# Attention, gate and output in one block, with later row sums for two chunks

## What is computed

```python
xn = _layernorm(x, axis=-1)
s = _L0_attn_ref(xn, wq, wk, wv, wo)     # softmax(q k^T * 32**-0.5, causal) v, then @ wo
g = _silu(_L0_ffn_ref(xn, W_base, b_base, W_router, lora_A, lora_B))
x = x + s * g                            # ffn: xn @ W_base.T + b + 2 * sum over top-2 experts w_e (xn A_e) B_e
```

## Time and profile before

| | us |
|---|---|
| median of 3 runs | 3402.35 (3400.29 to 3406.72) |
| the profiled execution | 3404.86 |
| its span, first to last instruction | 3403.1 |
| PE busy | 3266.6 |
| DVE busy | 1877.9 |
| ACT busy | 1441.0 |
| POOL busy | 1357.8 |

### The profile page before, as it was taken

The page is one execution under the profiler, slowest core; times in us unless marked ns, Lnnn a source line. Parts: engine busy times, 40 slices in busy tenths (PEclk is TensorE's granted clock), DMA queues, the critical chain, the costliest instruction groups (busy, mean ns, idle before and its releaser), DMA issues. The chain is left out here.

```text
span 3403.1 us, 51307 instructions
## 1 busy us (share of the span) xinstructions
PE 3266.6 (96%) x18048; PEld 2193.0 (64%) x18048; DVE 1877.9 (55%) x4622; ACT 1441.0 (42%) x2658; POOL 1357.8 (40%) x549
## 2 busy tenths in 40 slices
PE   6999999799999999999999999999997999989999
PEld 5888888655555555555555555555552788878887
DVE  5333332287777777777777777777771322223333
ACT  3221121046666666666666666666665211100000
POOL 0000000046766766776676677667666000000000
PEclk9999999899999999999999999999998999999999
DMA  6555554345665656566565656656664544435554
GB/s 229 161 161 159 171 175 143 110 97 123 131 143 124 140 128 135 128 136 143 122 139 130 137 131 131 139 128 137 134 150 114 176 147 140 140 130 194 196 188 171
DMA packets 283503, 494.53 MB, mean 145 GB/s; under 512 B 40864, under 2 KB 156576, under 8 KB 263328
## 3 DMA queue, kind: packets, MB, share of 16 engines
q1 hardware_dynamic: 260256, 333.04, 32.9%
q0 software_dynamic: 20736, 151.00, 22.1%
q10 hardware_dynamic: 2304, 7.87, 0.7%
HBM read 205.03 MB, written 134.74 MB: 100 GB/s over the span
## 5 line engine op out<-in xcount | busy, mean ns | idle before, releaser
L882 POOL TENSOR_TENSOR added<-added,probs 128x2048 f32<-128x2048 f32 (+3 forms) x320 | 1177.0, 3678 | 863.5 <-PE o_ps L953 812.4
L1061 DVE TENSOR_REDUCE row_max<-rows_ps 128x1 f32<-128x512 f32 x1536 | 994.1, 682 | 262.4 <-PE rows_ps L915 259.5
L1035 ACT ACTIVATE probs<-cols_ps 128x512 f32<-128x512 f32 x1728 | 922.3, 610 | 329.1 <-PE cols_ps L997 295.8
L1065 DVE CUSTOM_DVE_ANT_0 masked_rows<-rows_ps,tri 128x128 bf16<-128x128 f32 (+3 forms) x1024 | 482.1, 482 | 221.5 <-PE rows_ps L915 219.1
L915 PE MATMUL rows_ps<-k_st,q_st 96*128 96x512 f32 (+3 forms) x1536 | 527.0, 372 | 26.4 <-DMA q_st<-scratch_q_hi 17.0
L997 PE MATMUL cols_ps<-q_st,k_st 97*128 97x512 f32 x1248 | 519.6, 423 | 0.6
L953 PE MATMUL o_ps<-probs,v_st 128*32 128x512 f32 (+3 forms) x4224 | 429.4, 523 | 0.0
L997 PE MATMUL cols_ps<-q_st_last,k_st 97*128 97x512 f32 x928 | 382.5, 426 | 7.0 <-ACT dma_added L1035 3.1
L915 PEld LDWEIGHTS rows_ps<-k_st,q_st 96*128 96x128 f32 x1536 | 295.3, 193 | 117.0 <-DVE row_max L1061 46.3
L915 PE MATMUL rows_ps<-k_st,q_st_last 96*128 96x512 f32 (+3 forms) x1024 | 366.4, 384 | 2.7 <-DVE row_max L1061 0.4
L997 PEld LDWEIGHTS cols_ps<-q_st,k_st 97*128 97x128 f32 x1248 | 236.6, 190 | 171.2 <-issue 107.4
(11 more groups left out here) (113 smaller groups left out, 3799.9 us busy)
## 6 DMA issues: line engine op xcount, KB each, us to landing
dma_added<-probs POOLq DMA_DIRECT2D x144, 1024.0 KB, 7.4
q_st<-scratch_q_hi SPq DMA_DIRECT2D x96, 256.0 KB, 5.5
x_sb<-in_x SPq DMA_DIRECT2D x32, 512.0 KB, 3.9
scratch_xt_hi<-xt_hi SPq DMA_DIRECT2D x32, 512.0 KB, 6.0
scratch_xt_lo<-xt_lo SPq DMA_DIRECT2D x32, 512.0 KB, 6.7
scratch_q_hi<-out_hi SPq DMA_DIRECT2D x64, 256.0 KB, 2.4
scratch_q_lo<-out_lo SPq DMA_DIRECT2D x64, 256.0 KB, 2.9
l_sb<-scratch_l_inv SPq DMA_DIRECT2D x256, 64.0 KB, 4.3
```

The lines of the kernel that those rows point to most:

```text
L882: nc.gpsimd.tensor_tensor(total[:, :, q0:CH], total[:, :, q0:CH], probs_of(c, j)[:, :, q0:CH], ALU.add).then_inc(pool_added, 1)
L1035: nc.scalar.activation(probs_of(c, j)[:, :, i * P:(i + 1) * P], cols_ps[cols_slot(AT_T[t])][:, :].rearrange("p (h q) -> p h q", h=NREP), A ...
L1061: nc.vector.tensor_reduce(into, bank[:, :], AX.X, ALU.max).then_inc(rows_free, 1)
L1065: nc.vector.tensor_tensor_reduce(masked_rows[rows_slot(k)][:, 0:keys], bank[:, 0:keys], tri[:, CH - keys:CH], 1.0, MASKED, ALU.add, ALU.ma ...
```

## The change

1. **Row sums.** Y of chunks 1 and 2 stands at the second visit of the next chunk, eight tiles later; its normalisation keeps its distances. The semaphore of the adding DMAs is split by the chunk's parity.
2. **One block.** `attend`, `gate` and `output` become one block; the gate's and the output's programs are functions called by each engine behind its attention, or in the tail of it.
3. **Buffers.** The gate's and output's buffers are laid by hand over those of the attention. The split gate weights w[k] (high and low together) take the place of probs 0 to 6, added0 and dma_added0. l_inv is gone: the reciprocal is taken in place.
4. **Tail.** ACT rounds the gate weights at the start of the tail, each as soon as its score buffer is read. DVE makes the remainders and finishes tile 0's silu before the last reciprocal. PE makes tile 0's products before the last row sums. SP loads gate tile 0 in the last group, tile 1 when the last exponential is done, and everything else of the gate behind the tail.
5. **Gate to output.** The load and the split of output tile 0 stand before the last gate tile's silu; tile 1's load waits for the last gate product. The output uses two other banks.

```diff
-    _t = weighed_at((_c + 1) % CPB, 0 if _c else 2) + (0 if _c + 1 < CPB else NTG)
+    _t = weighed_at(_c + 1, 2) if _c + 1 < CPB else weighed_at(0, 0) + NTG
...
+        (ow_hi, o_x0, gw, ow_lo, ow_raw, g_g, o_raw0, g_t1, g_z, _, g_th, g_bias, o_g0) = laid_out(
+            ("ow_hi", [P, KT, D], FP32R), ("o_x0", [P, D], FP32),
+            ("gw", [P, NW, 2, D], FP32R),
...
@@ SP
+                if n.lin(1) == NG and c == 0:
+                    wait_apart(sp, probs_ready, n.lin(NUG, 0), passed)
+                    gate.load(sp, 1, 1)
...
+                            gate.load(sp, 0, 0)
...
             over_stages(run)
-            for s in range(CPB):
-                sp.wait_ge(o_stored[s], 16 + 16 * NG)
-            sp.wait_ge(gw_loaded, 16 * NW)
+            gate.stores_before_last(sp)
+            for s in o_stored:
+                wait_apart(sp, s, 16 + 16 * NG, passed)
+            output.load_first(sp)
+            gate.last_stores(sp, output.load_second)
+            output.loads_and_stores(sp)
@@ PE
                     elif kind == "Y":
+                        if n.lin(1) == NG:
+                            pe.wait_ge(rows_free, NSG * NG + 1)
+                            gate.first_products(pe)
                         row_sums(n, *op[1:])
             over_stages(run)
+            gate.products(pe)
+            output.products(pe)
@@ ACT
+            def split_high(n):
+                act.wait_ge(gw_loaded, 16 * NW)
+                for k in range(NW):
+                    if k < EARLY:
+                        j = next(j for c, j in reversed(RING) if probs_slot(RING.index((c, j))) == k)
+                        act.wait_ge(values_done, weighed_count(n, CPB - 1, 1, j))
+                        if j in ADDS[CPB - 1]:
+                            act.wait_ge(pool_added, n.lin(NADD, adds_through(CPB - 1, j) - NADD))
+                        if j in DMA_ADDS[CPB - 1]:
+                            act.wait_ge(dma_done[1], n.lin(16 * NDMA[1], 16 * (dma_adds_through(CPB - 1, j) - NDMA[1])))
+                    gate.high(act, k)
...
+            gate.tanhs(act, output.first_high)
+            output.highs(act)
@@ DVE
                     elif kind == "I":
                         cc, back = op[1:3]
+                        if n.lin(1) == NG:
+                            gate.lows(dve)
+                            gate.first_silu(dve, cols_full, cols_count(n, AT_Y[cc]))
                         dve.wait_ge(l_moved[cc % 2], n.lin(32, 16 * (cc // 2 + 1) - 32 * back))
-                        nc.vector.reciprocal(l_inv[cc % 2][:, :], l_few[cc % 2][:, :]).then_inc(l_inv_ready, 1)
+                        nc.vector.reciprocal(l_few[cc % 2][:, :], l_few[cc % 2][:, :]).then_inc(l_inv_ready, 1)
...
+            gate.silus(dve, output.first_low)
+            output.finishes(dve)
@@ in last_stores of the gate, SP
+        store(sp, Step(NPAIR - 1, 0))
+        wait_apart(sp, acc_full, 2 * NT, passed)
+        load_second(sp)
+        store(sp, Step(NPAIR - 1, 1))
```

More of the change, by code:

```diff
@@ L17 @@
+from collections import namedtuple
 from contextlib import ExitStack
@@ L552 @@
 NRG = len(RING)
+EARLY = 7
 def probs_slot(g):
@@ L645 @@
 NADD = sum(len(a) - 1 for a in ADDS if a)
-NDMA = sum(len(a) - 1 for a in DMA_ADDS if a)
+NDMA = [sum(len(a) - 1 for a in DMA_ADDS[par::2] if a) for par in range(2)]
 def adds_through(c, j):
@@ L676, in attend @@
         sb("gw_raw_end", [P, D])
+        probs = [sb(f"probs{i}", [P, NREP, CH]) for i in range(EARLY)]
+        added = [sb("added0", [P, NREP, CH])]
+        dma_added = [sb("dma_added0", [P, NREP, CH])]
+        probs += [sb(f"probs{i}", [P, NREP, CH]) for i in range(EARLY, NPROBS)]
+        added.append(sb("added1", [P, NREP, CH]))
+        dma_added.append(sb("dma_added1", [P, NREP, CH]))
         q_st.append(sb("q_st_last", [K1 + 1, NREP, CH], FP32R))
@@ L679, in attend @@
         v_st = [sb(f"v_st{i}", [P, S // P, HD]) for i in range(2)]
+        o_sb = [sb(f"o_sb{i}", [P, CH]) for i in range(CPB)]
+        g_t0 = sb("g_t0", [P, 2, NW, P], FP32R)
         ones = sb("ones", [P, HD])
-        probs = [sb(f"probs{i}", [P, NREP, CH]) for i in range(NPROBS)]
-        added = [sb(f"added{i}", [P, NREP, CH]) for i in range(2)]
-        dma_added = [sb(f"dma_added{i}", [P, NREP, CH]) for i in range(2)]
         row_max = [sb(f"row_max{i}", [P, NREP, TPC, CPB]) for i in range(2)]
@@ L710, in attend @@
         pool_added = sem("a_pool_added")
-        dma_done = sem("a_dma_done")
+        dma_done = [sem(f"a_dma_done{i}") for i in range(2)]
         chunk_copied = sem("a_chunk_copied")
@@ L720, in attend @@
         NW = KT + 1
+        gate = gate_programs(nc, ctx, sc, wo, b_base, gw_raw, gw, ow_raw, ow_hi, ow_lo, [g_t0, g_t1], g_bias, g_z, g_th, g_g,
+                             rows_ps[0:2], passed)
+        output = output_programs(nc, ctx, x, sc, out, ow_hi, ow_lo, [o_raw0, o_raw1], [o_t0, o_t1], [o_x0, o_x1], [o_g0, o_g1],
+                                 o_prod, o_y, rows_ps[2:4], gate, passed)
         block = ctx.enter_context(nc.Block())
@@ L809, in move_row @@
                 sp.dma_start(q_st[c][K1:K1 + 1, :, :].bitcast(FP32), row[c % 2][:, :]).then_inc(row_moved[c % 2], 16)
-            for s in o_stored:
+            for s in o_stored + gate.g_stored:
                 sp.sem_inc(s, 16)
@@ L821, in run @@
             def run(n, c, ops):
-                last_group = isinstance(n.pair, int) and n.lin(1) == NG - 1
+                last_group = n.lin(1) == NG - 1
+                if n.lin(1) == NG and c == 0:
+                    wait_apart(sp, probs_ready, n.lin(NUG, 0), passed)
+                    gate.load(sp, 1, 1)
                 for op in ops:
@@ L866, in run @@
                                          o_sb[cc][:, :]).then_inc(o_stored[cc], 16)
+                            if last_group and cc == 2:
+                                for i in range(2):
+                                    wait_apart(sp, o_stored[i], 16 + 16 * NG, passed)
+                                gate.load_bias(sp)
             over_stages(run)
-            for s in range(CPB):
-                sp.wait_ge(o_stored[s], 16 + 16 * NG)
-            sp.wait_ge(gw_loaded, 16 * NW)
+            gate.stores_before_last(sp)
[4 more added lines that the diff above has]
+            output.loads_and_stores(sp)
         @block.gpsimd
@@ L1010, in _ @@
             act.sem_inc(probs_ready, 1)
+            def split_high(n):
+                act.wait_ge(gw_loaded, 16 * NW)
+                for k in range(NW):
+                    if k < EARLY:
[6 more added lines that the diff above has]
+                    gate.high(act, k)
             def run(n, c, ops):
+                if n.lin(1) == NG and c == 0:
+                    split_high(n)
                 for op in ops:
```

513 lines of the change are left out of this document (252 added, 261 removed).

## The result

Over five runs the changed kernel takes 3381.26 us in the median (3374.66 to 3388.59), the kernel before, on the same chip, 3402.35 (3400.29 to 3407.04): the ratio on record, from all the runs, is 0.9925, with an interval of 0.9911 to 0.9939 (the two medians by themselves give 0.9938). It is faster by 21 us, where 57 were forecast, and 3381 lies above the range of 3334 to 3360. The profiled execution took 3379.06.

The account below looks back on a forecast made before the run. PE, busy 96% of the span, bounds the kernel, so only its waits and lower clock can be won. 26.6 + 25.4 - 8.4 + 13.5 = 57.1 us gained, forecasting 3345 us, range 3334 to 3360.

Parts of the forecast that it names:

- Part 1: Attention: later sums of chunks 1 and 2 remove PE's waits for POOL's adds; gain 26.6 us, bounds 18 to 29.
- Rival C: Attention: DVE waits at chunk 1's reciprocal behind SP's late move, stopping PE sixteen times; slower, 3412 us; chance 0.03.
- Part 2: From attention into gate: PE starts the gate's first products sooner, second gate tile at 2631.9; gain 25.4 us.
- Rival A: Gate start: DVE's first remainder held until POOL's last add ends, first product 4.4 us later; 3352 us; chance 0.30.
- Part 3: Gate: SP's late loads of tile 2 leave PE idle 6.2 us, then half clock; price 8.4 us, bounds 0 and 14.
- Part 4: From gate into output: the 11.3 us wait and half clock behind it go; gain 13.5 us, bounds 9 and 13.5.

Follow-up runs that it names:

- experiment 4: Changed kernel with the store of chunk 0's output six tiles later, so chunk 1's sums are sent ahead of it: 3350.14 us, 0.9834 of before.
- experiment 11: Kernel before, three blocks, with sums of chunks 1 and 2 eight tiles later, semaphore split, chunk 0's store six tiles later: 3374.22 us, 0.9900 of before.
- experiment 6: Changed kernel with chunk 1's normalisation (reciprocal and all that follows) two tiles sooner: 3418.95 us, 1.0046 of before.
- experiment 1: Changed kernel with chunk 1's sums back at the old place, chunk 2's still late: 3354.77 us, 0.9849 of before.
- experiment 7: Changed kernel with SP storing g of tile 0 and loading gate tile 2 before sending the last inverses: 3369.32 us, 0.9899 of before.
- experiment 8: Changed kernel with chunk 0's store six tiles later and gate tile 2 loaded before the last inverses are sent: 3338.91 us, 0.9806 of before.
- Experiment 9: Changed kernel with chunk 1's normalisation eight tiles later, plus two tiny DVE probe operations behind each copy of the attention's result: 3396.99 us, one run.
- experiment 2: Changed kernel with the sums of chunks 1 and 2 at their old places, so the one block alone: 3389.50 us, 0.9952 of before.

## Why the prediction was wrong

**Part 1 failed, and in one sentence of it:** "I cost these moves, and SP's, at nothing". The rest of the step was right. The waits for POOL went entirely, and experiments 4 and 11 show what the part is worth when nothing takes its place: 33 us in both. It was priced too low, at 26.6. The attention of experiment 4 takes 1813.4 (765.01 to 2576.06 + 2.36) where before has 1847.0, and of these 33.6 the forecast had the 25.0 of waits and 1.6 of clock. It bounded, but did not count, the waits for the row move, 2.7 before and 0.7 there. And it took a wait at the idleness shown for it: a score matmul's row lasts 0.39 where its neighbours start 0.23 apart, and the first one behind a wait is followed only after 0.31 (2633.89 to 2634.20), so a wait costs some 0.24 more than its idleness, fifteen times, 3.6. That makes 32.2; this splitting is worked out, not tested.

Against it stands DVE at the reciprocal: after less experiment 4 is 31 us by the medians, 34.9 in the attentions of the two traces. Its working: 12.7 of waits, 2.9 for twelve restarts, and half clock. By the granted clock the attention of after has seven lapses behind a stand, each 3.4 to 6.8 us long, 37.5 in all, of which PE spent some 34 working, so some 17 were lost. That makes 32.6. In the last group, with no stand, after has three more lapses of 3.4 us; their cause stays open, and they do not tell the two kernels apart, since experiment 4 has 10.2 us of half clock in its last group as well.

**Rival C** had the place, the order and the condition: SP's move behind the store of chunk 0, which waits for POOL, and a DVE that is in order. It was given 0.03 and 0.5 us a group, out of 7.45 us of landing less 7 of grace. The landing was right (7.2 at 1355.92), and two things were wrong. The grace was not 7 us but 5.0 (sent at 1355.92, DVE at the reciprocal at 1363.09 - 2.20 = 1360.89), since the sending itself stood behind POOL's product; 7.2 less 5.0 is the stand of 2.2. And the price of a stand is not its length, but its length and the half clock behind it. With these, 0.5 became 31 / 16, so 1.9 us a group, taken over all sixteen. The condition given for a loss, 3.6 a group, was worked out against 57 us; experiment 6, with 1.75 less of grace, was slower than before.

**Part 2, 22.0 for 25.4.** Rival A (0.30) was true in its mechanism. The remainders by tile (duration in ns, min/median/max), and POOL's last two adds:

```profile
L760 DVE TENSOR_TENSOR gw<-gw_raw,gw x9: 1209/1210/2858, 2611.8 to 2622.5; 128x1024 fp32r<-128x1024 f32 x9
```

```profile
2603.97 9.59 POOL L1223 TENSOR_TENSOR added<-added,probs 128x2048 f32<-128x2048 f32 x2
```

DVE's first remainder starts at 2611.78 and lasts 2.86 us, where its median is 1.21; POOL's last add ends at 2603.97 + 9.59 = 2613.56. That holds the remainder 1.65 us, and not the 4.4 of the rival, since POOL's last add ended 1.1 us behind the last weighing, where I had it 4.0 behind. So that the part came so near its forecast is in part luck: the forecast had no hold at all, and the hold happened to be short. PE idled 2.36 us, 1.5 more than forecast, and then ran some 3.4 at half clock. In experiments 1, 4, 7 and 8 nearly the full price of the rival shows, 3.8 us of idleness, since there the first remainder gets in between POOL's two last adds and the second is held. The hold seems to go both ways: in experiment 8, where a remainder gets in between them, the two adds take 10.64 us, in after 9.59. The section "SBUF: two separate sides" of the Trainium skill's page SBUF — State Buffer has it so. Experiment 9 agrees for DVE's side: of two operations of 15 elements only the one with two SBUF inputs was held, by up to 2.6 us; the one followed above was held to the end of the add. (The prediction's own rows put the first product at 2612.19 + 1.09 + 1.15 = 2614.4, not at 2614.7; this changes nothing.)

**Part 3, -11.5 for -8.4.** The order was read rightly: one wait for g_t, in front of the third tile, and a half clock behind it. It is 9.80 for 6.2. The first silu ended at 2637.2 for 2635.9, POOL took the product at 2643.94, the loads were issued at 2647.43 to 2649.25 for 2645.9, and the last landed at 2656.18, 6.9 us later for 4.5, in a stretch with a DMA share of 0.97: the stores of g, the output weights and the loads of tile 3 all came at once. Experiment 7 gives the 12 back.

**Part 4, 13.9 for 13.5**, as worked out, with no gap before the first output product.

**The range** held only A and small errors on top of it. C's place, 67 us above the forecast, was cut away as a point, where its mechanism has a scale: any price from 0.5 to 4 us a group was possible from the rows at hand, and the 1.9 found lies in its middle.

## What to carry to other kernels

When a stage is moved against the others, look at each in-order queue between the old and the new place for an instruction that now has to wait for a third engine; list for each what the next consumer has as grace, and give a stand its multiplier, the number of groups, and its clock. A tight chain of a small transfer is best cured at the queue, by putting what can wait behind what cannot: here one event moved by six tiles was worth 31 us. The joining of the three stages gave 24 in its own stretches (22.0 - 11.5 + 13.9), but 17 in the whole (experiment 2), since the attention became longer by 5.8. And if DVE must work with two SBUF inputs while GpSimd adds, put PE's first work on something that needs neither.

## What was new about the hardware

- A small transfer right behind large ones is late: 8 KB sent 0.6 us behind POOL's 1 MB, and 0.5 behind a store of 256 KB, were of use 7.2 us later, where the 8 KB of the inverses land in 1.4 in the median. No run parts the two neighbours, but one place in the trace of after speaks for the adding DMA: inverses sent at 2584.67, 0.85 behind an adding DMA (2583.82) and 9.5 behind the last store, were read back only at 2593.24, 8.6 later. Inverses sent 0.1 ahead of an adding DMA (2519.09) were read back after 1.5.
- DVE's operation with two SBUF inputs is held by an add of POOL that is under way, even with 15 elements a partition, and its recorded duration contains the hold (0.16 against up to 2.78 us).
- Lapses of the clock do not follow from the length of the idleness alone. 2.72 us before chunk 2's sums cost no clock in before, and a stand of 0.73 at 1123.89 cost none in after, yet a lapse follows the one of 0.35 below; sixteen weighings take 3.36 us behind it, and 1.92 elsewhere. What decides was not settled; in the last group lapses come with no stand at all. The stand of 0.35 in the timeline of PE:

```profile
1484.42 0.33 PE L1257 MATMUL rows_ps<-k_st,q_st 96*128 96x128 f32 x1 [0.35 <-DVE row_max L1432]
1484.67 3.36 PE L1295 MATMUL o_ps<-probs,v_st 128*32 128x512 f32 x16
```

- Small stands are expensive: twelve of them on PE, with 12.7 us together, cost the attention 31 to 35.
